# A second scratch buffer for the weight quantization of a Mamba-2 block's feed-forward stage

## The reference

```python
def _quantize(w):
    gamma = jnp.mean(jnp.abs(w))
    return jnp.clip(jnp.round(w / (gamma + EPS)), -1.0, 1.0)
def _bitlinear(x, w):
    return jnp.matmul(x, _quantize(w).T)
x1 = _bitlinear(x, w1)
x2 = _bitlinear(x, w2)
hidden = jax.nn.sigmoid(x1) * x2
return _bitlinear(hidden, w3)
...
x = x + _L0_attn_ref(_layernorm(x, axis=-1), ...)
x = x + _L0_ffn_ref(_layernorm(x, axis=-1), L0_ffn_w1, L0_ffn_w2, L0_ffn_w3)
```

## Time and profile before

| what | us |
|---|---|
| median of the 2 timed runs | 6222.77 |
| the 2 timed runs | 6026.63 and 6418.91 |
| the profiled execution | 6036.19 |
| its span on the slowest core (core 3) | 6034.6 |
| spans of its 8 cores | 6008.9 to 6034.6 |

### The profile page before, as it was taken

The page is one execution under the profiler, slowest core; times in us unless marked ns, Lnnn a source line. Parts: engine busy times, 40 slices in busy tenths (PEclk is TensorE's granted clock), DMA queues, the critical chain, the costliest instruction groups (busy, mean ns, idle before and its releaser), DMA issues.

```text
span 6034.6 us, 59575 instructions; the slowest of 8 cores (6008.9 to 6034.6 us)
## 1 busy us (share of the span) xinstructions
PE 4530.1 (75%) x21348; PEld 2253.8 (37%) x21348; DVE 2262.6 (37%) x2629; ACT 1477.4 (24%) x1787; POOL 572.2 (9%) x1090
## 2 busy tenths in 40 slices
PE   3875777778664677676776398777797665999997
PEld 1333555433221233332332144555543222444443
DVE  2555555412223333333333377556412323222112
ACT  1455333463002322323222112333321001000000
POOL 0001333100000000001000001333200000000000
PEclk8986555688876899888998698555598777999999
DMA  3894000384231534535334142000043321222222
GB/s 110 211 261 142 24 22 30 106 243 116 65 71 39 195 129 153 178 126 190 134 130 167 60 70 46 2 2 2 16 71 70 66 60 46 71 72 74 80 84 91
DMA packets 144885, 577.01 MB, mean 96 GB/s; under 512 B 36947, under 2 KB 39252, under 8 KB 106580
## 3 DMA queue, kind: packets, MB, share of 16 engines
q1 hardware_dynamic: 76468, 398.76, 20.0%
q0 software_dynamic: 68128, 174.44, 13.2%
HBM read 589.57 MB, written 85.98 MB: 112 GB/s over the span
## 4 chain that ended last, share of the span: by engine, by line
PE 61%; DVE 15%; DMA 12%; ACT 6%; issue 4%; POOL 1%; DVEq 0%; ACTq 0%; SPq 0%; POOLq 0%
PE p_ip L1043 11%; PE p_ip L1052 10%; PE p_ip L917 9%; PE p_ip L278 7%; PE p_ip L840 5%; PE p_w L1099 5%; PE p_ip L1099 5%; PE p_ip L731 4%; DMA aX_gslab<-w1T_t 3%; DVE aW_woslab L901 2%; DMA aX_gslab<-w3T_t 2%; DVE aW_tscr L379 1%; DMA aX_gslab<-w2T_t 1%; DVE STATES_bf L381 1%; PE p_ip L288 1%
## 5 line engine op out<-in xcount | busy, mean ns | idle before, releaser
L1043 PE MATMUL p_ip<-aH_h,aW_q 128*128 128x512 bf16 x2816 | 689.5, 408 | 459.0 <-DVE aW_q L1023 405.0
L917 PE MATMUL p_ip<-aA_xy,aW_woslab 128*128 128x512 bf16 x2048 | 526.0, 425 | 245.0 <-DVE aW_woslab L901 245.0
L1052 PE MATMUL p_ip<-aH_h,aW_q 128*128 128x512 bf16 x2816 | 622.1, 379 | 0.0
L1043 PEld LDWEIGHTS p_ip<-aH_h,aW_q 128*128 128x128 bf16 x2816 | 288.5, 104 | 853.0 <-issue 570.0
L278 PE MATMUL p_ip<-aW_stageR,aW_stageL 2*128 2x128 f32 x2048 | 511.0, 427 | 43.9 <-DMA aW_eacsrow<-aW_eacs 43.4
L278 PEld LDWEIGHTS p_ip<-aW_stageR,aW_stageL 2*128 2x128 f32 x2048 | 470.9, 325 | 106.1 <-issue 90.7
L1061 DVE TENSOR_TENSOR aA_hid<-aW_sig,p_ip 128x1024 bf16<-128x1024 f32 x88 | 107.5, 1221 | 1058.5 <-PE p_ip L1052 1048.2
L731 PE MATMUL p_ip<-aH_h,aW_wslab 128*128 128x512 bf16 x1536 | 367.0, 400 | 159.2 <-DMA aW_wslab<-winT_t 72.1
L1058 ACT ACTIVATE aW_sig<-p_ip 128x1024 f32<-128x1024 f32 x88 | 90.1, 1024 | 1540.8 <-PE p_ip L1043 1517.2
L917 PEld LDWEIGHTS p_ip<-aA_xy,aW_woslab 128*128 128x128 bf16 x2048 | 216.8, 107 | 554.2 <-issue 365.0
L1052 PEld LDWEIGHTS p_ip<-aH_h,aW_q 128*128 128x128 bf16 x2816 | 275.6, 98 | 332.2
(11 more groups left out here) (172 smaller groups left out, 6410.8 us busy)
## 6 DMA issues: line engine op xcount, KB each, us to landing
aW_wslab<-winT_t POOLq DMA_DIRECT2D x92, 512.0 KB, 6.1
aX_gslab<-w1T_t SPq DMA_DIRECT2D x44, 1024.0 KB, 7.5
aX_gslab<-w2T_t SPq DMA_DIRECT2D x44, 1024.0 KB, 5.4
aX_gslab<-w3T_t SPq DMA_DIRECT2D x44, 1024.0 KB, 7.2
aW_w1slab<-w1T_t SPq DMA_DIRECT2D x44, 1024.0 KB, 9.8
aW_w2slab<-w2T_t SPq DMA_DIRECT2D x44, 1024.0 KB, 6.0
aW_w2slab<-w3T_t SPq DMA_DIRECT2D x44, 1024.0 KB, 6.4
aW_woslab<-woutT_t POOLq DMA_DIRECT2D x32, 1024.0 KB, 8.3
```

The source lines that it names most:

```text
L917: ev_mm = P.add(T, lambda t, par=par, lh=lh, ec=ec, pb=pb: t.matmul(pb[lh][:, :], B["woslab"][par][:, 128 * ec:128 * ec + 128], B["xy"][:, ...
L1043: ex1 = P.add(T, lambda t, par=par, lh=lh, k=k: t.matmul(B["p_Y"][lh][:, :], B["q1"][par][:, 128 * k:128 * k + 128], B["h1"][:, k, 512 * l ...
L1052: ex2 = P.add(T, lambda t, par=par, lh=lh, k=k: t.matmul(B["p_diff"][lh][:, :], B["q2"][par][:, 128 * k:128 * k + 128], B["h1"][:, k, 512 ...
```

## The change

A second scratch buffer `qtmp2` of the same size is allocated behind `q3l` in overlay A, in memory that the feed-forward stage does not use otherwise. A counter `qti` runs over all uses of the scratch; even uses take `qtmp`, odd ones `qtmp2`. The last reader is kept per buffer, so that each writer waits for the last reader of its own buffer. With three uses per tile, the use ahead of the one before is: for w1 the w2 of the tile before, for w2 the w3 of the tile before, for w3 the w1 of the same tile.

```diff
     B["q3l"] = arA.alloc("q3l", [128, FFN_R, 2048], BF16)
+    B["qtmp2"] = arA.alloc("qtmp2", [128, 2048], BF16)
...
-        qtmpf = [None]
+        qtmpf = [None, None]
+        qti = [0]
...
+                    qi = qti[0] % 2
+                    qti[0] += 1
+                    qb = B["qtmp"] if qi == 0 else B["qtmp2"]
...
-                        ea2 = P.add(V, lambda v, w=wslabs[par], tc=tcol: v.tensor_scalar(
-                            B["qtmp"][:, :], w[:, :], B["tpp"][:, tc:tc + 1], None, ALU.is_gt),
-                            waits=[qtmpf[0]])
+                        ea2 = P.add(V, lambda v, w=wslabs[par], qb=qb, tc=tcol: v.tensor_scalar(
+                            qb[:, :], w[:, :], B["tpp"][:, tc:tc + 1], None, ALU.is_gt),
+                            waits=[qtmpf[qi]])
...
-                        ea = P.add(A, lambda a, w=wslabs[par], tc=tcol: a.activation(
-                            B["qtmp"][:, :], w[:, :], AF.Sign, bias=B["tneg"][:, tc:tc + 1]),
-                            waits=[d_, qtmpf[0], ev_gamma_done[0]])
+                        ea = P.add(A, lambda a, w=wslabs[par], qb=qb, tc=tcol: a.activation(
+                            qb[:, :], w[:, :], AF.Sign, bias=B["tneg"][:, tc:tc + 1]),
+                            waits=[d_, qtmpf[qi], ev_gamma_done[0]])
...
-                    qtmpf[0] = eq
+                    qtmpf[qi] = eq
...
-                    ec_ = P.add(A, lambda a, par=par: a.activation(
-                        B["qtmp"][:, :], B["w3slab"][par][:, :], AF.Sign, bias=B["tneg"][:, 2:3]),
-                        waits=[d3, qtmpf[0]])
+                    ec_ = P.add(A, lambda a, par=par, qb=qb: a.activation(
+                        qb[:, :], B["w3slab"][par][:, :], AF.Sign, bias=B["tneg"][:, 2:3]),
+                        waits=[d3, qtmpf[qi]])
...
-                    qtmpf[0] = eq3
+                    qtmpf[qi] = eq3
```

More of the change, by code:

```diff
@@ L1010, in quant @@
                             waits=[d_, qf[0], qf[1], qcache_done.get(tcol), ev_gamma_done[0]])
-                        ea2 = P.add(V, lambda v, w=wslabs[par], tc=tcol: v.tensor_scalar(
-                            B["qtmp"][:, :], w[:, :], B["tpp"][:, tc:tc + 1], None, ALU.is_gt),
-                            waits=[qtmpf[0]])
-                        eq = P.add(V, lambda v, q=qbufs[par]: v.tensor_tensor(
-                            q[:, :], B["qtmp"][:, :], q[:, :], ALU.subtract))
-                    else:
-                        ea = P.add(A, lambda a, w=wslabs[par], tc=tcol: a.activation(
-                            B["qtmp"][:, :], w[:, :], AF.Sign, bias=B["tneg"][:, tc:tc + 1]),
-                            waits=[d_, qtmpf[0], ev_gamma_done[0]])
+                        ea2 = P.add(V, lambda v, w=wslabs[par], qb=qb, tc=tcol: v.tensor_scalar(
+                            qb[:, :], w[:, :], B["tpp"][:, tc:tc + 1], None, ALU.is_gt),
+                            waits=[qtmpf[qi]])
+                        eq = P.add(V, lambda v, q=qbufs[par], qb=qb: v.tensor_tensor(
+                            q[:, :], qb[:, :], q[:, :], ALU.subtract))
+                    else:
+                        ea = P.add(A, lambda a, w=wslabs[par], qb=qb, tc=tcol: a.activation(
+                            qb[:, :], w[:, :], AF.Sign, bias=B["tneg"][:, tc:tc + 1]),
+                            waits=[d_, qtmpf[qi], ev_gamma_done[0]])
                         eb = P.add(A, lambda a, q=qbufs[par], w=wslabs[par], tc=tcol: a.activation(
@@ L1022, in quant @@
                             waits=[qf[0], qf[1], qcache_done.get(tcol)])
-                        eq = P.add(V, lambda v, q=qbufs[par]: v.tensor_tensor(
-                            q[:, :], q[:, :], B["qtmp"][:, :], ALU.add),
+                        eq = P.add(V, lambda v, q=qbufs[par], qb=qb: v.tensor_tensor(
+                            q[:, :], q[:, :], qb[:, :], ALU.add),
                             waits=[ea, eb])
-                    qtmpf[0] = eq
+                    qtmpf[qi] = eq
                     wf[par] = eq
@@ L1075, in build_program @@
                         waits=[q3lf[li], qcache_done.get(2)] + (mam_bar if ri == 0 and li < 2 else []))
-                    eq3 = P.add(V, lambda v, li=li: v.tensor_tensor(
-                        B["q3l"][:, li, :], B["q3l"][:, li, :], B["qtmp"][:, :], ALU.add),
+                    eq3 = P.add(V, lambda v, li=li, qb=qb: v.tensor_tensor(
+                        B["q3l"][:, li, :], B["q3l"][:, li, :], qb[:, :], ALU.add),
                         waits=[ec_, eb3])
-                    qtmpf[0] = eq3
+                    qtmpf[qi] = eq3
                     w3f[par] = eq3
```

## The result

| what | before | after |
|---|---|---|
| time, median of all timed runs (us) | 6038.43 | 6007.32 |
| ratio after to before, with its 95% interval | | 0.9935 [0.992, 0.995] |
| profiled execution (us) | 6036.19 | 6000.81 |
| span of its slowest core (us) | 6034.6 (core 3) | 5999.3 (core 6) |

The changed kernel is faster by 0.65%, some 39 us (30 to 48 by the interval), which is within 2%. The forecast was 5989, or 47 us less than before; the range, 5945 to 6042, holds the time. The median of before now rests on ten runs, the one shown ahead of the prediction on two. In some runs of either kernel the cores of one die, sometimes of both, ran at a lower granted clock and took longer; the ratios leave these runs out.

The account below looks back on a forecast made before the run. The prediction saw the feed-forward stage bound by a 23.9 us chain through scratch, ACT, DVE and PE, with the shared slab close behind; 50 + 4 = 54 us by means, 47 stepped through: 6036.19 - 47 = 5989 us, range 5945 to 6042.

Parts of the forecast that it names:

- the two loops: Feed-forward stage: after the change a step takes the later of a two-step loop (22.3 us) and the slab alone (22.1).
- the slab loop: Chain through the slab shared by w2 and w3, from one w3 add to the next: 22.1 us a step.
- the loop through PE: Path from L1073's end through w1's quantization, PE and L1061 to the next w3 add: 23.85 us, part of the two-step loop.
- the whole 3.2 us (5914): Rival: every one of 38 steps saves L1017's full 3.2 us earlier start, 122 us in all; chance 0.06.
- nothing (6036): Rival: L1017 waits for the w1 load instead, so the time stays 6036; chance of nothing gained 0.08.
- 22.3 to 22.9: Sign of a right forecast: us per step in rounds two to six, computed as 22.6 against 24.2 before.
- The q1s term: Cost of w1's write-back falling inside the w2 load's flight: taken as 0, with up to 0.9 us seen for q3s.
- the two-step loop: Loop through PE (23.85 us) and then the slab (20.73), serving two steps: 44.6 / 2 = 22.3 us a step.
- the rival of colder starts: L1043 at 10.00 us throughout, on PE's lower clock: 28 us saved, 6008; chance 0.17 together with partial q1s cost.
- the scatter that the forecast had put at 7 us: Stage's steps: stepping through tiles with their own load and L1043 times gave 47 us saved, against 54 by means.
- The stretches behind the stage only shift: Sign of a right forecast: what runs after the feed-forward stage moves in time only.
- the 54 ahead of it: Saving by mean values: 50 us over 31 steps of rounds two to six plus 4 in round one.

Follow-up runs that it names:

- e3: Changed kernel, both scratch buffers kept, with the first Sign of w1 again waiting for the w3 add of the tile before; ratio to before 0.9992, step 24.24 us.
- e1: Changed kernel plus a slab of its own for w3; first set without interval (step 20.38 us), repeated at ratio to before 0.9807, step 20.41.
- e7: Changed kernel, shared slab kept, with the next tile's w1 quantization emitted ahead of the sigmoid; ratio to before 0.9907, step 22.85 us.
- e4: Changed kernel with the write-back q1s issued only once the w2 load has landed; ratio to before 0.9908, step 22.71 us against 23.05.
- e6: Changed kernel plus own slab for w3 and the next tile's w1 quantization ahead of the sigmoid; ratio to before 0.9406, step 14.58 us.

## Why the prediction was right, and where it was off

**The wait and what stands behind it: right.** L1022 starts 0.15 us behind L1081 on the mean (0.1 forecast), and e3 shows that this wait is all of the change. The limit moved to the two loops, as computed: PE's wait fell to 6.98 us ("about 7"), 21 of the 44 adds of w3 on core 6 wait for the slab, e1 removes the slab loop and gets 20.4, and e7 removes the loop through PE and gets 22.85. Neither the whole 3.2 us (5914) nor nothing (6036) came; the w1 load held L1022 in only 5 tiles of core 6 besides the entry, for 2.5 us together.

**The sum of the steps: 47.0 us, as forecast, though its terms were not.** Rounds two to six took 22.99 each instead of 22.6, just outside "22.3 to 22.9", and saved 37.7; round one saved 9.3 instead of 4. What was mis-sized:

- The q1s term, "I take 0". It measures 0.34 us a step (e4), 13 us in all, of which 11 fall into rounds two to six. The one late q3s beside a load of 5.1 was a single case and misled. By the Trainium skill (DMA: Bandwidth & Descriptors, section Issuing engines are not separate DMA queues), SP's and GpSimd's transfers share the DMA engines and interleave; e4 bears that out, with 0.2 us for the w2 load where q3s had suggested up to 0.9. The forecast's test, a median more than 0.3 from 6.0, was too coarse: 0.2 on the w2 load and 0.2 on the w3 load are 0.4 in a loop that both pass through.
- "L1043 takes about 0.2 more on the mean than the 8.37". It takes 9.09, that is 0.7 more. Before, it took 8.68 already, 0.3 over the 8.37; beyond that it is 0.41, half of it in each step of the two-step loop: 0.2 x 38 = 8 us. This was the rival of colder starts, about a third of the way from 8.68 to 10.00. Why the first matmuls run at the lower level more often, though the wait ahead of them is shorter than before (6.98 against 8.70), the rows don't say.
- The loads, in round one above all. All were taken from the slowest core before, core 3. For round one that gave 6.8 and 7.4; the means over the 8 cores were 6.3 and 6.4 before, and are 6.2 and 6.3 after. On core 6 after the medians are 6.1 and 6.6:

```profile
aW_w2slab<-w2T_t SPq DMA_DIRECT2D x8, 1024.0 KB, 6.1
aW_w2slab<-w3T_t SPq DMA_DIRECT2D x7, 1024.0 KB, 6.6
```

In rounds two to six core 3 gave medians of 6.0 and 6.4, 12.4 for the two. The means over the 8 cores were 5.94 and 5.82, or 11.8, before, and are 6.16 and 6.07, or 12.2, after. So the 0.4 that the early q1s adds only brings the loads close to what the forecast had counted: an error that hid the other.

With the measured loads and L1048 put into the forecast's loops, the two-step loop comes to (44.6 + 0.7 + 0.2) / 2 = 22.8 a step; the measured 22.99 leaves 0.2 for the scatter that the forecast had put at 7 us over 38 steps, 0.2 each.

**"The stretches behind the stage only shift", and the steps between rounds with them: wrong for the latter, by 5.0 us.** Their work is unchanged, but the first matmuls of L1107 now run at the lower clock at about half of the 40 round ends of the 8 cores, against 4 of 40 before. L1107's matmuls of a round take 56.3 us on the mean in place of 55.6, which is 3.8 of the 5.0; what makes up the rest is open. Two round ends of core 1 after:

```profile
2112.38 3.31 PE L1107 MATMUL p_w<-aA_hid,aA_q3l 128*128 128x512 bf16 x8 [2.87 <-DVE aA_q3l L1084]
...
2823.43 1.89 PE L1107 MATMUL p_w<-aA_hid,aA_q3l 128*128 128x512 bf16 x8 [2.87 <-DVE aA_q3l L1084]
```

and the windows around their starts (columns as above):

```profile
2112.00:2116.00 4.00, 3.62 (x11) 1.35 (x12) 0.37 (x2) 1.06 (x1) 0.53 (x1) 0.59 0.72 154
2823.00:2827.00 4.00, 3.57 (x17) 1.68 (x18) 0.98 (x2) 2.96 (x2) 0.53 (x1) 1.00 0.68 158
```

The wait ahead is 2.87 us both times; the granted clock is 0.59 behind one and 1.00 behind the other, and the same 8 matmuls take 3.31 and 1.89 us. In e3, with the old wait back, the steps between rounds return to 373.8.

So 47.0 less 5.0 is 42.0 in the stage, and the kernel's ratio stands for 39 of it. That the steps came to 47.0, the very forecast, is luck: the errors nearly cancelled, and loads counted too long, in round one above all, paid for part of the write-back and the colder matmuls. The 7 us that the forecast took off for scatter came from stepping through the tiles, which the rows don't show; the 54 ahead of it can be followed.

## What to carry to other kernels

When a wait is removed, count the time to the next limit, not the length of the wait: two loops only 0.2 us apart (22.3 and 22.1 us a step by the forecast) stood here behind 3.3 us of waiting. The scratch buffer alone was worth 0.65%, the slab alone nothing, both 2%, and both with a reordered list 6%. A transfer that moves into the flight of another can have a price even where a single row shows none, here 0.34 us a step; sum it over every load of the loop that ends last. Look for list order, too: an operation that waits for a far engine holds all that stand behind it, and moving one quantization ahead of it, once the slab was free, was the largest gain of all.

## What was unexpected of the hardware

The same wait of 2.87 us left PE at full clock in one place and at 0.59 of it in another, as shown above, so the wait just ahead does not settle the clock by itself. And a shorter wait made L1048 slower: 9.09 us after 6.98 us of idleness on the mean, against 8.68 after 8.70. In e1 the steps were shorter still, PE waited 4.42 us, and L1049 stayed at 9.1. In e7 the product behind the wait, now L1059, took 9.21 after 6.82, and L1050 right behind it 7.07; only with PE nearly continuous (e6) did both come down to 7.07 to 7.09. What the clock follows here is left open.
